# First layer of a two-layer attention and expert kernel: who adds the two parts of the rotation, and who copies the turned sums

## The chip, the cores and the metric

The kernel runs on one core of one Trainium2 chip. The metric is the device time of one execution in microseconds (us). The engines of the core are TensorE (PE in the profile; its weight loads are PEld), VectorE (DVE), ScalarE (ACT), GpSimd (POOL) and SyncE (SP, which here only issues DMAs). Each engine works through its own list of instructions in order; they wait for each other through semaphores.

## The reference: what is computed

The input is 16 sequences ("batches") of 512 tokens with 128 channels, float32. Two layers follow, each of the form `x = x + attention(layernorm(x)) + ffn(layernorm(x))`:

```
layer 1 attention: q, k, v = xn Wq', xn Wk', xn Wv'   (16 heads of 8 channels)
                   q, k = rope(q), rope(k);  q, k = elu(q)+1, elu(k)+1
                   y_t = q_t (sum_{s<=t} k_s v_s') / max(q_t . sum_{s<=t} k_s, 1e-6);   y Wo'
layer 1 ffn:       router softmax over 8 experts, the best two, weights renormalised,
                   squared-ReLU expert MLPs (128-512-128), plus one shared MLP
layer 2 attention: softmax attention over chunks of 64 with a gate from a two-step dynamics
layer 2 ffn:       token-shifted blend, squared ReLU, sigmoid gate
```

The change touches only layer 1's attention. The rotation (rope) of the projected queries and keys is computed as `x * cos + swapped(x) * sin`, where `swapped(x)` comes from a second projection with permuted weights. Its sum goes on to `elu(.)+1`, computed as `max(x, 0) + exp(-relu(-x))`. The attention output carries a ninth column for each head, the denominator; the quotient of the two is what is multiplied by Wo.

## The kernel before, in words

The program has three stages: the first layer over 16 batches (some 16 equal rounds, from about 42 us to 511 us), the expert tiles, and the second layer. Only the first stage is of interest here. In it all engines run a software pipeline: `body(b, first, last)` of each engine is called for b = 0 to 15, and while batch b's attention is computed, the front of batch b+1 (projection, rotation, feature map, router) and the layer norm of batch b+2 are mixed in. The order on each engine is written out by hand; nothing else plans it.

**TensorE, in the order of one round b** (line numbers of the profile): scores of sheet 0 (L1760; a sheet is a group of heads), the wide part of sheets 0 and 1 (`attend_wide`, L1779), the turn of `xn` of b+1 (L1688), half of the output projection of b-1 (L1851, L1852), scores 1, values of sheet 0 (`attend_narrow`, L1788), projections of q for b+1 (L1703, L1704), scores 2, values 1, projections of k for b+1, scores 3, the other half of the projection of b-1, v of b+1 (L1713), wide part of sheets 2 and 3, values 2, turn of k (`turn_k`, L1734), turn of the first attention sums (`turn_oT(b, 0)`, L1820), `sum_states` (L1745), values 3, the shared MLP's first product in four parts (L1837), between which stand `turn_oT(b, 1)` (L1820), `prefix` of the router (L1725) and `turn_y` (L1826).

**VectorE**: `cut` multiplies the scores of four PSUM banks by the causal mask (L1198, four instructions for each sheet); `rotate(b+1, c)` comes after the cuts of sheets 1 (c = 0, queries) and 2 (c = 1, keys): two products out of PSUM (L1071, L1073) and then their sum `t1 + t2` in SBUF (L1076, 128x512 float32). After the cut of sheet 3 comes `feature` (L1095, twice), which needs ScalarE's exponential of the sum; then `residual`, `logits_out`, `router_max`, `ln(b+2)` (L1065), `router`, `y_out(b, 0)` (L1203), `states` (L1084), `router_pick`, `y_out(b, 1)` (L1203), `normalise` (L1209 to L1213) and `slots`. `y_out` copies the turned sums from PSUM bank W7 to `yb` in SBUF, 128x288 float32; `normalise` needs both halves and makes `y`, which TensorE's `turn_y` waits for. The next `prefix` in TensorE's list also waits for both halves (L1721), since it writes to W7.

**ScalarE**: `evac_xnT`, `exps(b+1, 0)` (L809 and L811: the two activations behind the rotation's sum, waiting for semaphore `rot`), `evac_oT(b, 0)`, `exps(b+1, 1)`, `evac_v`, two of `sheets_of_k`, `exp_router`, `evac_ktok` (L860), two more of `sheets_of_k`, `evac_oT(b, 1)` (L840), and four times `square_h` (L850 ReLU, L854 square), with `evac_yT` before the last.

**GpSimd**: eight indirect DMAs a round write the normalised rows of batch b to the experts' places (`scatter`, L687), two after the first scores of the round, two after `pv_done` says that values 0 are done; then `ln_root(b+2)` (L667 to L679, seven small instructions; not issued for the last two batches); then two scatters after values 1, and two at the end of the round's scores. `ln(b+2)` on VectorE overwrites `xn` of batch b, so it waits until all eight scatters of b have landed:

```
if not early(n, 2) and first_layer:
    dve.wait_ge(scattered[n.p], n.own(16 * 2 * J, 0))      # L1063
```

The functions that the diff touches, and what calls them:

Of the kernel before, what the change touches and what calls it, by code (L numbers as in the profile page):

```python
# [9 lines left out]
ALU = mybir.AluOpType  # L10
# [5 lines left out]
H, DH = 16, 8  # L16
E, FF = 8, 512
NB = FF // 128
J = T // 128
CHUNK = 64  # L20
SHEETS, G = 4, 4
PAIRS, TWO = SHEETS // 2, 2
# [84 lines left out]
def build(nc, io, out):  # L107
    ctx = ExitStack()
    with ctx:
# [20 lines left out]
        OT, W5, W6, W7 = bank[4], bank[5], bank[6], bank[7]  # L130
# [186 lines left out]
        def early(b, d):  # L317

            return b.less(d)
# [336 lines left out]
        def _(pool):  # L656
# [24 lines left out]
            def scatter(n, ks):  # L681

                written = value(pool, n.at(1, 1))
                pool.wait_ge(consts_loaded, 16 * CONSTS)
                pool.wait_ge(slots_ready, written)
                for k in ks:
                    nc.gpsimd.indirect_dma_start(  # L687
                        xs_d[:, :], bass.IndirectOffsetOnAxis(ap=idx[n.p][:, k:k + 1], axis=0),
                        xn[n.p][:, k % J, :], None).then_inc(scattered[n.p], 16)

            def body(b, first, last):
                pool.wait_ge(a_ps, b.at(H, G))
                scatter(b, range(0, 2))
                pool.wait_ge(pv_done, b.at(SHEETS, 1))
                scatter(b, range(2, 4))
                if b.known() + 2 < B:
                    ln_root(b + 2)
                pool.wait_ge(pv_done, b.at(SHEETS, 2))
                scatter(b, range(4, 6))
                pool.wait_ge(a_ps, b.at(H, H))  # L700
                scatter(b, range(6, 2 * J))

# [92 lines left out]
        def _(act):  # L795
# [40 lines left out]
            def evac_oT(b, a):  # L836
# [2 lines left out]
                    act.wait_ge(oTT_ps, b.at(PAIRS, a - 1))  # L839
                nc.scalar.copy(oT[a][:, :], OT[:, :]).then_inc(oT_sb, 1)  # L840

            def evac_yT(b, first_layer=True):
                act.wait_ge(yT_ps, b.at(1, 1))
                nc.scalar.copy(yT[:, :], (OT if first_layer else W6)[:, :]).then_inc(yT_sb, 1)  # L844
# [24 lines left out]
            def body(b, first, last):  # L869
                if not last:  # L870
                    evac_xnT(b + 1)
                    exps(b + 1, [0])
                evac_oT(b, 0)
                if not last:
                    exps(b + 1, [1])
                    evac_v(b + 1)
                    sheets_of_k(b + 1, range(2))
                    exp_router(b + 1)
                    evac_ktok(b + 1)
                    sheets_of_k(b + 1, range(2, SHEETS))  # L880
                evac_oT(b, 1)
                for k in range(NB):
                    square_h(b, k)
                    if k == 2 and not last:
                        evac_yT(b)

# [149 lines left out]
        def _(dve):  # L1036
# [31 lines left out]
            def rotate(n, c):  # L1068

                dve.wait_ge(qk_ps, n.at(2, c + 1))  # L1070
                nc.vector.tensor_tensor(t1[c][:, :], W5[:, :], rope[:, 0, :], ALU.mult).then_inc(rot_cos, 1)  # L1071
                dve.wait_ge(qkp_ps, n.at(2, c + 1))
                nc.vector.tensor_tensor(t2[c][:, :], W6[:, :], rope[:, 1, :], ALU.mult).then_inc(rot_sin, 1)  # L1073
                dve.wait_ge(rot_cos, n.at(2, c + 1))
                dve.wait_ge(rot_sin, n.at(2, c + 1))
                nc.vector.tensor_tensor(t1[c][:, :], t1[c][:, :], t2[c][:, :], ALU.add).then_inc(rot, 1)  # L1076

            def states(n):

# [307 lines left out]
            def body(b, first, last):  # L1387
                more = b.known() + 2 < B
                if last:
                    counts()  # L1390
                cut(b, 0)
                if more:
                    dve.wait_ge(x_loaded[b.p], (b + 2).own(16, 16))
                    ln_moments(b + 2)
                slot_weights(b)
                if last:
                    bounds(0)
                    inside(0)
                cut(b, 1)
                if not last:  # L1400
                    rotate(b + 1, 0)
                cut(b, 2)
                if last:
                    row_terms(0)
                    expert_terms()
                if not last:
                    rotate(b + 1, 1)
                cut(b, 3)
                if last:
                    first_tiles()  # L1410
                if not last:
                    feature(b + 1)
                if not first:
                    residual(b + -1)
                if not last:
                    logits_out(b + 1)
                    router_max(b + 1)
                if more:
                    ln(b + 2)
                if not last:  # L1420
                    router(b + 1)
                y_out(b, 0)
                if not last:
                    states(b + 1)
                    router_pick(b + 1)
                y_out(b, 1)
                if not last:
                    normalise(b)
                    slots(b + 1)
# [784 lines left out]
```

## Time and profile before

| | us |
|---|---|
| median of 3 runs (1529.15 to 1532.43) | 1532.0 |
| the profiled execution's own time | 1530.86 |
| its span | 1529.0 |
| TensorE busy in the span | 1415.1 (93%) |
| VectorE busy | 1179.3 (77%) |
| ScalarE busy | 818.9 (54%) |
| GpSimd busy | 524.4 (34%) |

Times in the rows are us from the start of the span, durations are us unless marked ns, and `xN` is a count. A row of a timeline gives start, duration, engine, line, operation, output and input, and in brackets how long the engine was idle before it and what ended that. The ends of matmuls are modelled, so neighbouring PE rows overlap: the distance from start to start tells more than the duration. PEclk is the granted clock of TensorE as a share of 2.4 GHz.

### The profile page before, as it was taken

Reading aid. Unit: us, or ns where it says so; the run is one execution under the profiler, and the core shown is the slowest. Engines: PE = TensorE matmul, PEld = TensorE weight load, DVE = VectorE, ACT = ScalarE, POOL = GpSimd, SP = SyncE. Lnnn points to the kernel's source line nnn. Section 1 sums busy time; section 2 is a strip of 40 time slices with the busy share of each in tenths; the row PEclk is TensorE's granted clock in tenths of the full one; section 3 lists DMA queues with packets and bytes.
Section 4 is the critical chain, followed back from the end, with each engine's and each line's share of the span. In section 5 each row is a group of like instructions: output and inputs, shape, how many; then the busy total and the mean of one; then the engine's idle time right before and its main releaser. Section 6 shows DMA issues by size and latency. Waiting matters only on the chain.

```text
span 1529.0 us, 35462 instructions
## 1 busy us (share of the span) xinstructions
PE 1415.1 (93%) x12938; PEld 914.1 (60%) x12952; DVE 1179.3 (77%) x2690; ACT 818.9 (54%) x1565; POOL 524.4 (34%) x943
## 2 busy tenths in 40 slices
PE   3899999999998799999998999999999999999994
PEld 1667667667677699998885444444444444444432
DVE  3899889889888496456677788888888888888752
ACT  2344434534533333334434677777667777776672
POOL 2343333333233011162412244444444444442121
PEclk8899999999998899999999999999999999999996
DMA  4111111111111566776974343343344443432300
GB/s 121 40 42 56 47 40 58 45 42 56 38 37 36 160 211 209 213 249 209 269 201 78 91 104 99 93 105 93 85 102 105 103 101 94 104 89 71 81 9 14
DMA packets 119084, 152.86 MB, mean 100 GB/s; under 512 B 31348, under 2 KB 83700, under 8 KB 114292
## 3 DMA queue, kind: packets, MB, share of 16 engines
q1 hardware_dynamic: 105992, 120.25, 28.9%
q0 software_dynamic: 12928, 30.43, 6.9%
q8 instruction: 101, 1.65, 0.5%
q14 instruction: 63, 0.52, 0.1%
HBM read 109.01 MB, written 41.09 MB: 98 GB/s over the span
## 4 chain that ended last, share of the span: by engine, by line
PE 49%; DVE 32%; POOL 6%; issue 5%; ACT 5%; SPq 2%; DMA 1%; POOLq 0%; DVEq 0%; ACTq 0%
PE bank L1935 8%; PE bank L1926 8%; DVE P L1198 8%; DVE nmax L1503 8%; PE bank L1803 5%; PE bank L1981 5%; PE bank L2004 4%; ACT P L939 3%; PE bank L1760 2%; PE bank L1837 2%; PE bank L1944 2%; PE bank L1851 2%; DVE t L1073 1%; DVE t L1071 1%; PE bank L2051 1%
## 5 line engine op out<-in xcount | busy, mean ns | idle before, releaser
L1503 DVE TENSOR_REDUCE nmax<-bank 128x1 f32<-128x512 f32 (+3 forms) x704 | 428.6, 633 | 87.7 <-PE bank L1981 86.9
L939 ACT ACTIVATE P<-bank 128x512 f32<-128x512 f32 x640 | 371.3, 599 | 186.0 <-PE bank L2004 179.8
L1981 PE MATMUL bank<-KT,QT 76*128 76x512 bf16 (+3 forms) x1024 | 252.2, 304 | 28.8 <-DVE nmax L1503 20.4
L2004 PE MATMUL bank<-QT,KT 78*128 78x512 bf16 (+3 forms) x1024 | 246.1, 303 | 9.0 <-ACT P L939 5.6
L687 POOL DMA_INDIRECT xs_d<-xn,idx x128 | 124.5, 972 | 308.0 <-PE bank L1760 218.5
L1981 PEld LDWEIGHTS bank<-KT,QT 76*128 76x128 bf16 x1024 | 87.4, 97 | 188.2 <-DVE nmax L1503 129.4
L1803 PE MATMUL bank<-P,V 128*32 128x512 f32 (+3 forms) x2048 | 193.1, 450 | 0.0
L1198 DVE TENSOR_TENSOR P<-bank,early_w 128x512 f32<-128x512 f32 x256 | 158.6, 680 | 37.9 <-PE bank L1760 37.8
L903 ACT ACTIVATE hr<-bank 128x512 f32<-128x512 f32 x144 | 86.0, 597 | 177.9 <-PE bank L1926 174.9
L735 POOL DMA_INDIRECT hT<-ys_d,idx x104 | 103.5, 995 | 162.4 <-PE bank L2004 133.8
L1467 DVE TENSOR_TENSOR hT<-hr 128x512 f32<-128x512 f32 x144 | 98.0, 691 | 68.3 <-ACT hr L903 67.6
L2004 PEld LDWEIGHTS bank<-QT,KT 78*128 78x128 bf16 x1024 | 99.0, 98 | 86.0 <-ACT P L939 30.8
L1935 PEld LDWEIGHTS bank<-P,hT 128*128 128x128 f32 x1152 | 139.0, 192 | 7.4 <-issue 3.0
L1926 PE MATMUL bank<-P 128*128 128x256 f32 x576 | 139.5, 386 | 1.8 <-issue 1.8
L1935 PE MATMUL bank<-P,hT 128*128 128x128 f32 x1152 | 140.5, 275 | 0.7 <-DVE P L1473 0.6
L723 POOL DMA_DIRECT2D ys_d<-P x72 | 52.4, 727 | 225.0 <-DVE P L1473 218.8
L1926 PEld LDWEIGHTS bank<-P 128*128 128x128 f32 x576 | 106.7, 194 | 14.8 <-issue 2.4
L809 ACT ACTIVATE t<-t 128x512 f32<-128x512 f32 x32 | 20.2, 631 | 159.5 <-DVE t L1076 159.5
L1760 PEld LDWEIGHTS bank<-P,QT 32*128 32x128 f32 x2048 | 65.9, 192 | 45.1 <-issue 43.3
L1760 PE MATMUL bank<-P,QT 32*128 32x128 f32 x2048 | 77.8, 290 | 7.6 <-DVE P L1198 7.5
L1803 PEld LDWEIGHTS bank<-P,V 128*32 128x32 f32 x2048 | 40.7, 108 | 64.4 <-issue 49.6
L1851 PE MATMUL bank<-early_w,hT 128*128 128x128 f32 x512 | 70.3, 281 | 1.9 <-ACT yT L844 1.9
(257 smaller groups left out, 2227.2 us busy)
## 6 DMA issues: line engine op xcount, KB each, us to landing
P<-in_fc SPq DMA_DIRECT2D x72, 256.0 KB, 2.9
P<-in_proj SPq DMA_DIRECT2D x72, 256.0 KB, 3.5
QT<-parts_d SPq DMA_DIRECT2D x96, 192.0 KB
parts_d<-parts SPq DMA_DIRECT2D x32, 384.0 KB, 2.7
P<-xs_d SPq DMA_DIRECT2D x72, 128.0 KB, 3.0
ys_d<-P POOLq DMA_DIRECT2D x72, 128.0 KB, 3.6
KT<-parts_d SPq DMA_DIRECT2D x64, 128.0 KB
KT<-parts_d SPq DMA_DIRECT2D x32, 192.0 KB
```

Source lines behind the costliest of these rows:

```text
L687: nc.gpsimd.indirect_dma_start(xs_d[:, :], bass.IndirectOffsetOnAxis(ap=idx[n.p][:, k:k + 1], axis=0), xn[n.p][:, k % J, :], None).then_in ...
L735: nc.gpsimd.indirect_dma_start(gathered_rows(n)[:, k, :], None, rows, bass.IndirectOffsetOnAxis(ap=idx[n.p][:, k:k + 1], axis=0)).then_inc ...
L939: nc.scalar.activation(P[s % 2][:, u, :], bank[k % 2][:, :], ACT.Exp, scale=float(DH) ** -0.5).then_inc(s_sb, 1)
L1198: nc.vector.tensor_tensor(P[s % 2][:, g, :].rearrange("p (j c) -> p j c", c=128), bank[g][:, :].rearrange("p (j c) -> p j c", c=128), tri[ ...
L1503: nc.vector.tensor_reduce(nmax[:, s // TWO, h:h + TWO * nh - 1:TWO, j], max_bank(n, k)[:, 0:nh * w].rearrange("p (h w) -> p h w", h=nh), A ...
L1760: ins = pe.matmul(bank[g][:, tile], kS[b.p][quad, s, tile], qf[b.p][quad, tile], start=True, stop=True)
L1803: ins = pe.matmul(OT[32 * g:32 * g + 32, 128 * kb:T], values(b, kb, s, g), P[s % 2][:, u, c:c + n], start=(s % TWO == 0 and k == 0), stop= ...
L1851: pe.matmul(o, hT[:, j // 2, k, c0:c0 + 128], spj[:, k, :], start=(k == 0), stop=False)
L1926: ins = pe.matmul(w[:, i * GT:(i + 1) * GT], wfc[t.p][:, c * 128:(c + 1) * 128], xgT[t.p % 2], start=True, stop=True)
L1935: ins = pe.matmul(bank[6][:, c * 128:(c + 1) * 128], hT[:, t.p % 2, k, c * 128:(c + 1) * 128], wpj[t.p][:, k, :], start=(k == 0), stop=(k ...
L1981: ins = pe.matmul(max_bank(n, k)[:, i * w:(i + 1) * w], QT[n.p][0:MROWS, h, j * 128:(j + 1) * 128], KT[n.p][0:MROWS, h, 0:w], start=True, ...
L2004: ins = pe.matmul(bank[k % 2][:, c:c + n], KT[b.p][0:SROWS, h, 128 * kb:128 * kb + 128], QT[b.p][0:SROWS, h, 128 * kb:T], start=True, stop ...
```

## The change

`rotate` issues its sum on VectorE for the first batch only. For the others GpSimd does it in `sum_rotation(b+1, c)`: c = 0 behind `ln_root(b+2)`, c = 1 behind the scatters 4 and 5. The copies of the turned sums go to ScalarE: `copy_y(b, 0)` stands behind `evac_ktok(b+1)`, `copy_y(b, 1)` behind the first `square_h` of the round.

```
# GpSimd
+            def sum_rotation(n, c):
+                pool.wait_ge(rot_cos, n.at(2, c + 1))
+                pool.wait_ge(rot_sin, n.at(2, c + 1))
+                nc.gpsimd.tensor_tensor(t1[c][:, :], t1[c][:, :], t2[c][:, :], ALU.add).then_inc(rot, 1)
             def body(b, first, last):
...
                 if b.known() + 2 < B:
                     ln_root(b + 2)
+                if not last:
+                    sum_rotation(b + 1, 0)
                 pool.wait_ge(pv_done, b.at(SHEETS, 2))
                 scatter(b, range(4, 6))
+                if not last:
+                    sum_rotation(b + 1, 1)
                 pool.wait_ge(a_ps, b.at(H, H))
                 scatter(b, range(6, 2 * J))
# ScalarE
+            def copy_y(b, a):
+                act.wait_ge(oTT_ps, b.at(PAIRS, a + 1))
+                nc.scalar.copy(yb[0][...same places...], W7[...]).then_inc(y_sb, 1)
...
                     evac_ktok(b + 1)
+                copy_y(b, 0)
+                if not last:
                     sheets_of_k(b + 1, range(2, SHEETS))
                 evac_oT(b, 1)
                 for k in range(NB):
                     square_h(b, k)
+                    if k == 0:
+                        copy_y(b, 1)
# VectorE
-                dve.wait_ge(rot_cos, n.at(2, c + 1))
-                dve.wait_ge(rot_sin, n.at(2, c + 1))
-                nc.vector.tensor_tensor(t1[c][:, :], t1[c][:, :], t2[c][:, :], ALU.add).then_inc(rot, 1)
+                if early(n, 1):
+                    (the same three lines)
...
-                y_out(b, 0)
                 if not last:
                     states(b + 1)
                     router_pick(b + 1)
-                y_out(b, 1)
```

## Rows read from the trace of the kernel before

**Rows 1.** Busy time by stretch: one round (stretch, length; PE, PEld, DVE, ACT, POOL busy; PEclk, DMA).
```profile
244.32:273.30 28.98, 28.08 (x379) 20.54 (x379) 25.61 (x69) 13.34 (x25) 9.98 (x15) 1.00 0.16 48
```

**Rows 2.** Timeline of TensorE: the end of one round, then the next one.
```profile
241.40 0.49 PE L1725 MATMUL bank<-pickb,before 128*128 128x8 bf16 x14 [0.43 <-DVE yb L1203]
...
242.87 0.66 PE L1826 MATMUL bank<-ident,y 128*128 128x128 f32 x4
...
244.32 1.17 PE L1760 MATMUL bank<-P,QT 32*128 32x128 f32 x32
...
257.26 1.17 PE L1760 MATMUL bank<-P,QT 32*128 32x128 f32 x32 [0.18 <-DVE P L1198]
...
262.39 1.08 PE L1788 MATMUL bank<-P,V 128*32 128x128 f32 x32
263.61 0.52 PE L1734 MATMUL bank<-ident,t 128*128 128x128 f32 x3
...
264.70 1.77 PE L1745 MATMUL bank<-V,P 128*128 128x144 f32 x12
...
268.39 0.63 PE L1820 MATMUL bank<-ident,oT 128*128 128x128 f32 x4
268.86 1.08 PE L1837 MATMUL bank<-xnT,early_w 128*128 128x512 f32 x2
```

**Rows 3.** Timeline of VectorE over the same stretch.
```profile
242.12 0.69 DVE L1213 TENSOR_TENSOR y<-yb,rden 128x512 f32<-128x512 f32 x1
...
245.58 2.48 DVE L1198 TENSOR_TENSOR P<-bank,early_w 128x512 f32<-128x512 f32 x4 [1.88 <-PE bank L1760]
...
258.42 0.69 DVE L1076 TENSOR_TENSOR t<-t 128x512 f32<-128x512 f32 x1
259.03 2.47 DVE L1198 TENSOR_TENSOR P<-bank,early_w 128x512 f32<-128x512 f32 x4
...
262.02 0.68 DVE L1095 SCALAR_TENSOR_TENSOR t<-t,ee 128x512 f32<-128x512 f32 x1
...
263.83 1.11 DVE L1065 TENSOR_SCALAR xn<-xt,mv,rstd 128x128 f32<-128x128 f32 x4
...
268.17 0.60 DVE L1084 TENSOR_TENSOR P<-bank,own 128x432 f32<-128x432 f32 x1
```

**Rows 4.** Timeline of ScalarE over the same stretch.
```profile
259.14 0.63 ACT L809 ACTIVATE t<-t 128x512 f32<-128x512 f32 x1 [2.62 <-DVE t L1076]
...
268.57 0.60 ACT L850 ACTIVATE hr<-bank 128x512 f32<-128x512 f32 x1 [0.44 <-PE bank L1837]
```

**Rows 5.** Timeline of GpSimd over the same stretch.
```profile
256.21 0.20 POOL L679 TENSOR_TENSOR rstd<-rstd,std 128x4 f32<-128x4 f32 x1
256.95 1.03 POOL L687 DMA_INDIRECT xs_d<-xn,idx  x1 [0.54 <-issue]
258.30 0.95 POOL L687 DMA_INDIRECT xs_d<-xn,idx  x1 [0.30 <-issue]
```

**Rows 6.** Groups of GpSimd's instructions by line and shape (busy us, mean ns of one).
```profile
L671 POOL TENSOR_TENSOR std<-std,rstd 128x4 f32<-128x4 f32 x32 | 6.4, 200 | 2.5
...
L428 POOL TENSOR_TENSOR fhn<-fhn 128x64 f32<-128x64 f32 x15 | 4.8, 320 | 1.3
```

**Rows 7.** Timeline near the start: a GpSimd instruction, then the VectorE one beside it.
```profile
20.71 0.54 POOL L679 TENSOR_TENSOR rstd<-rstd,std 128x4 f32<-128x4 f32 x1
...
20.50 0.69 DVE L1076 TENSOR_TENSOR t<-t 128x512 f32<-128x512 f32 x1
```

**Rows 8.** DMA issues by line (count, median us from issue to landing).
```profile
xs_d<-xn,idx POOLq DMA_INDIRECT x128, 2.2
```

**Rows 9.** Timeline of TensorE in round 0.
```profile
59.37 0.52 PE L1734 MATMUL bank<-ident,t 128*128 128x128 f32 x3 [1.71 <-DVE lg L1101]
...
60.96 2.94 PE L1745 MATMUL bank<-V,P 128*128 128x144 f32 x12 [0.63 <-ACT P L860]
```

**Rows 10.** Timeline of TensorE behind the last round.
```profile
506.61 1.16 PE L1851 MATMUL bank<-early_w,hT 128*128 128x128 f32 x8 [1.86 <-ACT yT L844]
```

More of the change, by code:

```diff
@@ L840, in evac_oT @@
                 nc.scalar.copy(oT[a][:, :], OT[:, :]).then_inc(oT_sb, 1)
+            def copy_y(b, a):
+                act.wait_ge(oTT_ps, b.at(PAIRS, a + 1))
+                nc.scalar.copy(yb[0][:, :, TWO * G * a:TWO * G * (a + 1), :].rearrange("p j (g b) c -> p j g (b c)", b=TWO),
+                               W7[:, :].rearrange("p (j g c) -> p j g c", j=J, g=G)[:, :, :, 0:TWO * (DH + 1)]).then_inc(y_sb, 1)
             def evac_yT(b, first_layer=True):
@@ L1073, in rotate @@
                 nc.vector.tensor_tensor(t2[c][:, :], W6[:, :], rope[:, 1, :], ALU.mult).then_inc(rot_sin, 1)
-                dve.wait_ge(rot_cos, n.at(2, c + 1))
-                dve.wait_ge(rot_sin, n.at(2, c + 1))
-                nc.vector.tensor_tensor(t1[c][:, :], t1[c][:, :], t2[c][:, :], ALU.add).then_inc(rot, 1)
+                if early(n, 1):
+                    dve.wait_ge(rot_cos, n.at(2, c + 1))
+                    dve.wait_ge(rot_sin, n.at(2, c + 1))
+                    nc.vector.tensor_tensor(t1[c][:, :], t1[c][:, :], t2[c][:, :], ALU.add).then_inc(rot, 1)
             def states(n):
```

## The prediction

> **What bounds the kernel now.** I first split the span by the busy time of its stretches, then read one round of the first layer in the chain of waits, and last the timeline of each engine over that round. The rounds repeat to a hundredth of a us, so one will do for all: 28.98 us long, at full clock, 2.4 GHz, with TensorE marked busy for 28.08 and VectorE for 25.61 [rows 1]. The reader should see there that both are nearly full: whatever is taken off VectorE can give back only the time in which TensorE waits for it. The chain of waits runs along VectorE from the first cut of a round to the copy of the second half of the turned sums, and along TensorE from there to the next round. TensorE's own waits in a round are few. It waits 0.18 at the fourth scores for a cut, and 0.2 at the turn of k: 262.39 to 263.61 is 1.22, where the same 32 products take 1.01 elsewhere, between neighbours whose starts follow directly. It waits 0.3 at `sum_states`, for ScalarE's copy of the turned k. It waits 0.43 at `prefix`, for the copy in question, and 0.1 at `turn_y` [rows 2]. Together that is some 1.2 to 1.5 us of 28.98. So the largest gain that the change could have, with every wait gone, is 15 rounds by 1.5, 22 us; the question is what new waits it brings.
>
> **What is removed.** VectorE loses two sums of 0.69, with the two waits ahead of each some 0.75 a piece [rows 3], and two copies, which by their effect on the next start are worth 0.38 and 0.47: 2.35 us a round. Its first benefit is at the cuts: the third cut starts at once when its scores are there, so the fourth scores start 0.18 earlier, at 257.08. VectorE's cuts start 1.26 after the scores that they wait for (244.32 to 245.58) and four take 2.4 to the next start, so `feature` for the queries could start at 257.08 + 1.26 + 2.4 = 260.74, where the fourth cut before alone began at 259.03 [rows 2, 3].
>
> **What the GpSimd add costs.** No row shows a 128x512 add there. GpSimd adds 128x4 in 0.20 and multiplies or adds 128x64 in 0.32 [rows 6], which makes 0.12 for 60 elements, 2.0 ns for one, and for 512 elements 0.20 + 508 x 0.0020 = 1.2 us. The bounds are 0.32 (the shorter instruction; below that nothing argues) and 2.2 (twice the slope). I take 1.2 as the line through two rows of the same operation. The Trainium skill, GPSIMD Engine Reference, section 3.1, gives about 2.6 cycles an element at 1.2 GHz for two inputs against VectorE's one; by its figures the add would be an estimated 1.1 us plus the dispatch, close to the value from the rows.
>
> **Where the adds stand.** This is the point of the case. GpSimd's list is in order, and the adds have been put behind work that ends late. `ln_root` ends at 256.41 and the products of the queries' rotation have long been ready, so the first add runs from 256.42 to 257.62. The fourth scatter follows after the same 0.54 as now, at 258.16, the fifth 1.35 later at 259.51, ending at 260.46 [rows 5]. The second add then runs from 260.50 to 261.70. VectorE used to end the same sum at 258.42 + 0.69 = 259.11, and ScalarE took it up at 259.14 [rows 3, 4]. So ScalarE's two activations on the keys, which the list holds ahead of V's copies, start at 261.74 instead of 259.14; their results are there 1.29 later, and VectorE's second `feature` starts at 263.07 instead of 262.02 [rows 3]. That is 1.05 late, although VectorE itself stood ready 1.3 us early. The delay of the queries' sum (by 2.9 us) costs nothing: its exponential is done at some 259.0, before `feature` at 260.74, and `evac_oT(b, 0)` behind it is not needed before TensorE's second wide part, after 261.
>
> **What follows the late feature.** Its chain is residual, logits, the turn of k, ScalarE's sheets and its copy of the turned k, `sum_states`. None of these can start without it, and nothing else in the chain became shorter. TensorE's `turn_k` moves from 263.61 to 264.66 and `sum_states` from 264.70 to 265.75; TensorE, idle before the former for 0.2 now, is idle for about 1.4. `turn_oT(b, 1)` moves from 268.39 to 269.44 and the second shared product could start 0.47 later, at 269.91 [rows 2].
>
> **The scatters' second effect.** GpSimd's scatters 6 and 7 move behind the late add, to 262.24 and 263.50, and scatters land 2.2 after their issue [rows 8]: 265.70. VectorE's `ln(b+2)` waits for them. It would be ready at 263.83 + 1.05 = 264.88 [rows 3], so it waits 0.85 more and is 1.9 late. Here the two removed copies pay: `states` comes at 268.17 + 1.9 - 0.38 = 269.69 and ends at 270.29, which holds the second shared product until 270.35 instead of 269.91; `prefix` is then possible at 271.32.
>
> **The copies on ScalarE.** The first stands in a free stretch and has TensorE's turn long behind it; nothing waits for it but `turn_oT(b, 1)`, 3 us later. The second stands behind the ReLU and the square of the first shared product: the ReLU starts at 268.57 + 1.05 = 269.62 [rows 4], the square ends 1.29 later, the copy takes 0.45 (a 128x288 piece beside the 128x512 ReLU's 0.60; bounds 0.3 and 0.6) and is done at some 271.25. Before, it was done 0.15 ahead of `prefix` (241.40), thus at 270.23 in this round. `prefix` moves from 270.38 to 271.40, and `normalise` behind the copy takes the same 1.56 to the end of `y` (241.25 to 242.81) [rows 2, 3], so `turn_y` and the next round's first scores move by the same 1.05, to within 0.05. The three paths (states, router's pick, copy) arrive nearly together; no second delay adds up.
>
> **The sum.** A round is 1.05 longer. This holds for rounds 0 to 13: 14.7 us. Round 14 has no `ln_root`, and the adds are early: there TensorE loses 0.45 of its waits and still waits for the late copy; I count 0.5 gained. In the last round no rotation is left, and TensorE waits for ScalarE at the end (1.86 before 506.61) [rows 10], whose list is longer by one copy that matters: 0.4 lost. That is 14.6. One more term: in round 0, TensorE stood 1.71 and 0.63 us idle at just these two places, and then its clock fell to 1.2 GHz: `sum_states` took 2.94 instead of 1.77, and the values behind it were longer too, 1.6 together [rows 2, 9]. The changed kernel stands idle for about 1.4 and 0.3 there in each round. That is less, so I expect the fall in few rounds, and count one beyond round 0: 1.6. In all 16.2. The profiled execution took 1530.9 by its own clock (its span is 1529.0), which makes 1547.1; the median of the runs shown is 1.1 above it, 1532.0, which makes 1548.2. Forecast: 1548. Its own range, with the add at 1.0 to 1.4 and none to four falls of the clock, is 1541 to 1556.
>
> **Rivals.**
> 1. VectorE gets in first. An instruction of GpSimd that began 0.21 after VectorE's sum of two SBUF tiles took 0.54 instead of 0.20, ending just behind it [rows 7]: the two exclude each other. Here the second add would begin at 260.50 and `feature` of the queries, with two inputs in SBUF, at 260.74. If the add comes first, `feature` waits, which is harmless. If GpSimd is a quarter us slower, it waits for `feature` until 261.41, and each round is 0.9 longer again: 14 x 1.95 - 0.1 + two falls of the clock 3.2 = 30.4, 1562. For it: the margin is 0.24 with an add that no row shows. Against it: 0.24 is over the scatter of the rows. (The Trainium skill, SBUF — State Buffer, section "Who interferes with whom", says that a VectorE instruction with two SBUF inputs and a GpSimd one that reads SBUF exclude each other and the first holds the port; the trace agrees, by the same 0.54. With the rule as with the row the sum is the same.)
> 2. The clock falls in each round: 14 x (1.05 + 1.6) - 0.1 = 37, 1569. For it round 0 [rows 9], against it that its idle time was 0.6 us longer, and the 1.86 idle before 506.61, behind which eight products took 1.16, no longer than at full clock [rows 10].
> 3. The other side, faster: GpSimd's add is short enough. `feature` of the keys starts at 260.67 plus twice the add; that equals today's 262.02 with an add of 0.67, and from there down the round gets shorter, until at 0.33 TensorE and ScalarE's late copy bind, and a round is 0.5 shorter: 15 x 0.5 = 7.5, 1524. For it: 0.67 is VectorE's own time for the sum. Against it: the two rows' slope makes 1.2, and 0.67 would need less than half of that slope.
> 4. The delays find slack that I missed (the keys' path loses 1.05 but the waits of 0.18, 0.2, 0.43 go), and the time is the same: 1530 to 1534.
>
> **How the numbers follow.** Forecast 0.60; rival 1, 0.12; rival 2, 0.09; rival 3, 0.11; rival 4, 0.08. A measurement of this kernel tells 0.2%, 3 us, from no change. Slower holds the forecast and rivals 1 and 2, 0.81; faster 0.11; same 0.08. The range must leave out no more than 0.2: I let go of rivals 3 and 4, and it reaches up into rival 2: 1538 to 1567.
>
> **What would show it.** In the profile after: GpSimd's add near 1.2 us (step 1); ScalarE's L809 for the keys waiting for POOL, not DVE, and starting some 17.4 us after the round's first scores instead of 14.8 (step 2); VectorE idle before its second `feature`, and idle before `xn` for a DMA; TensorE idle over 1 us before the turn of k; rounds of 30.0 us, and 28.5 for round 14. I am wrong if the add is under 0.7, if the second add begins before the scatters 4 and 5 are through, or if rounds are 31 and more with the clock at 0.5 behind the turn of k.

## The result, and the profile after

The changed kernel took 1548.74 us (median of 4 runs, 1544.8 to 1549.73) against 1532.22 for the kernel before on the same chip (4 runs, 1529.15 to 1533.01): a ratio of 1.011, 95% interval 1.0089 to 1.013. It is slower, by 16.5 us where 16.2 were forecast. The profiled execution has a span of 1548.0 us against 1529.0, 19.0 more. Its busy times are TensorE 1414.6 us, VectorE 1159.5 (19.8 less), ScalarE 826.8 (7.9 more), GpSimd 572.1 (47.7 more).

One round of the changed kernel, as its stretch (the columns are those of [rows 1]; scores to scores):

```profile
252.62:282.75 30.13, 28.00 (x378) 20.64 (x378) 24.38 (x65) 13.78 (x27) 13.02 (x17) 1.00 0.15 45
```

30.13 us instead of 28.98, at the same full clock. VectorE is marked busy for 1.23 us less in it (although one of its products, held by GpSimd's add, counts 0.64 more), TensorE for 0.08 less, and yet the round is 1.15 longer. Now the timeline of TensorE in the same round. To compare with [rows 2], take 8.30 off the starts: that round began at 244.32, this one at 252.62.

```profile
252.62 1.17 PE L1778 MATMUL bank<-P,QT 32*128 32x128 f32 x32
...
265.31 1.17 PE L1778 MATMUL bank<-P,QT 32*128 32x128 f32 x32
...
272.69 0.52 PE L1752 MATMUL bank<-ident,t 128*128 128x128 f32 x3 [1.17 <-DVE lg L1121]
...
273.78 1.77 PE L1763 MATMUL bank<-V,P 128*128 128x144 f32 x12
...
278.77 1.12 PE L1855 MATMUL bank<-xnT,early_w 128*128 128x512 f32 x2 [0.72 <-DVE P L1104]
279.74 0.49 PE L1743 MATMUL bank<-pickb,before 128*128 128x8 bf16 x14
...
281.31 0.65 PE L1844 MATMUL bank<-ident,y 128*128 128x128 f32 x4
...
282.75 1.17 PE L1778 MATMUL bank<-P,QT 32*128 32x128 f32 x32
```

The 0.18 ahead of the fourth scores is gone (265.31), and so is the 0.43 ahead of `prefix` (L1743). Two longer waits stand in their place: 1.17 at the turn of k, and 0.72 at the second shared product, for VectorE's `states` (L1104). VectorE in that stretch:

```profile
268.98 1.32 DVE L1115 SCALAR_TENSOR_TENSOR P<-t,ee 128x512 f32<-128x512 f32 x1
271.09 0.69 DVE L1115 SCALAR_TENSOR_TENSOR t<-t,ee 128x512 f32<-128x512 f32 x1 [0.80 <-ACT ee L821]
...
274.13 1.12 DVE L1084 TENSOR_SCALAR xn<-xt,mv,rstd 128x128 f32<-128x128 f32 x4 [1.14 <-DMA xs_d<-xn,idx]
...
278.11 0.61 DVE L1104 TENSOR_TENSOR P<-bank,own 128x432 f32<-128x432 f32 x1
```

VectorE stands idle twice, for 0.80 and 1.14 us: time that it used to spend on the sums and copies. The GpSimd list that makes it wait, and ScalarE between the two:

```profile
264.68 1.28 POOL L695 TENSOR_TENSOR t<-t 128x512 f32<-128x512 f32 x1
266.12 1.04 POOL L687 DMA_INDIRECT xs_d<-xn,idx  x1 [0.16 <-issue]
267.46 0.96 POOL L687 DMA_INDIRECT xs_d<-xn,idx  x1 [0.31 <-issue]
268.45 1.28 POOL L695 TENSOR_TENSOR t<-t 128x512 f32<-128x512 f32 x1
269.90 1.25 POOL L687 DMA_INDIRECT xs_d<-xn,idx  x1 [0.17 <-issue]
271.46 1.16 POOL L687 DMA_INDIRECT xs_d<-xn,idx  x1 [0.30 <-issue]
```

```profile
269.77 0.63 ACT L819 ACTIVATE t<-t 128x512 f32<-128x512 f32 x1 [2.01 <-POOL t L695]
...
278.82 0.38 ACT L854 COPY yb<-bank 128x288 f32<-128x288 f32 x1
```

The waits of the whole trace, by engine and line (us in total, times, longest), show that this is every round and not this one:

```profile
DVE xn L1084 <- DMA xs_d<-xn,idx: 16.3, 14, 1.6
```

### The profile page after: what moved, and what is told of

Read it like the earlier page. It is cut to its first block, busy times and chain, and to the rows that moved or that the text cites. A ratio compares the mean times of both kernels' runs of the same rounds, so it can differ in the third digit from the quotient of the medians.

```text
span 1548.0 us, 35462 instructions
## 1 busy us (share of the span) xinstructions
PE 1414.6 (91%) x12952; PEld 914.2 (59%) x12952; DVE 1159.5 (75%) x2628; ACT 826.8 (53%) x1597; POOL 572.1 (37%) x973
## 4 chain that ended last, share of the span: by engine, by line
PE 52%; DVE 23%; POOL 10%; issue 5%; ACT 4%; DMA 3%; SPq 2%; POOLq 0%; DVEq 0%; ACTq 0%
DVE nmax L1521 9%; PE bank L1953 8%; PE bank L1944 8%; PE bank L1821 7%; PE bank L1999 6%; PE bank L2022 5%; POOL xs_d L687 4%; PE bank L1778 3%; POOL t L695 2%; ACT P L958 2%; DMA xs_d<-xn,idx 2%; PE bank L1962 2%; PE bank L1869 2%; PE bank L1806 1%; PE bank L2069 1%
## 5 line engine op out<-in xcount | busy, mean ns | idle before, releaser
L687 POOL DMA_INDIRECT xs_d<-xn,idx x128 | 131.9, 1030 | 278.1 <-PE bank L1778 196.8
L1218 DVE TENSOR_TENSOR P<-bank,early_w 128x512 f32<-128x512 f32 x256 | 159.0, 684 | 47.9 <-PE bank L1778 47.7
L1855 PE MATMUL bank<-xnT,early_w 128*128 128x512 f32 x128 | 70.6, 636 | 9.3 <-DVE P L1104 9.3
```

Of the source, the lines that this page charges most:

```text
L687: nc.gpsimd.indirect_dma_start(xs_d[:, :], bass.IndirectOffsetOnAxis(ap=idx[n.p][:, k:k + 1], axis=0), xn[n.p][:, k % J, :], None).then_in ...
L1218: nc.vector.tensor_tensor(P[s % 2][:, g, :].rearrange("p (j c) -> p j c", c=128), bank[g][:, :].rearrange("p (j c) -> p j c", c=128), tri[ ...
```

## Experiments

All ratios are to the kernel before, run in between on the same chip. The kernels ran on three chips, and these differ: before took 1530.79 us on chip 1, 1539.15 on chip 2 and 1541.99 on chip 3. The pair of the result (1532.22) is like chip 1, so the runs there bear on it most directly; what the other chips add of their own is taken up with their runs. The runs on chip 2 came first, and the expectations for chip 1 refer to them.

### On chip 1: before, after, and both late paths taken away

**The kernel before, traced once more.**

> The kernel before itself, for its trace on the chip of these runs. The kernel with the copies alone showed rounds of 29.76 us against 28.98 in the trace of before, and yet took 1.0007 of the time of before on its chip. Theory A (the copies cost 0.78 us a round, and something of like size is saved or spent outside the rounds): here again rounds of 28.98 to 29.0 us, the fourth group of cuts 0.0 us idle. Theory B (a wait of about 0.7 us before the fourth group of cuts, TensorE's scores named, belongs to the execution or the chip and not to the copies): rounds of 29.6 to 29.8 here as well, with that wait in them.

Measured: rounds of 28.96 to 28.99 us, one execution of 1531.5 us, and no wait ahead of the fourth cuts. So the wait seen with the copies alone (below) is not in the kernel before on this chip; for the others the question stays.

**The changed kernel, once more.**

> The changed kernel itself, beside its parts on one chip. Both theories: rounds of 30.13 us in the trace and 1.010 to 1.013 of the time of before. If the adds alone (31.0 us rounds, 1.0098) and the whole change come out the same here, the copies bring nothing.

Measured: 1546.56 us, ratio 1.0107 (1.0086 to 1.0129), rounds of 30.1 us. The result repeats.

**A third buffer of rows, and the second add ahead of scatters 4 and 5.** The buffer lies in a part of `P[1]` that the first layer doesn't use; `ln(b+2)` then waits for the scatters of b-1, long landed.

```
-        xn = [sb(...) for p in range(2)]
+        xn = [sb(...) for p in range(2)] + [P[1][:, UNITS - 1, :].rearrange(...)]
+        rows_of(n): xn[n.known() % 3] in the first layer, xn[n.p] as before behind it
+                                                     # used by scatter, ln and the turn of xn
-                if not early(n, 2) and first_layer:
-                    dve.wait_ge(scattered[n.p], n.own(16 * 2 * J, 0))
+                if not early(n, 3) and first_layer:
+                    old = n + -3
+                    dve.wait_ge(scattered[old.p], old.own(16 * 2 * J, 16 * 2 * J))
...
-                pool.wait_ge(pv_done, b.at(SHEETS, 2))
-                scatter(b, range(4, 6))
                 if not last:
                     sum_rotation(b + 1, 1)
+                pool.wait_ge(pv_done, b.at(SHEETS, 2))
+                scatter(b, range(4, 6))
```

> The whole change, with both late paths taken away: a third buffer of normalised rows, so that the fourth next message's rows wait for no scatter, and the second add ahead of scatters 4 and 5, so that it starts when its products are there. Theory of two late paths (landing of the scatters, and the keys' activation behind the second add): with both gone the round is 28.5 us, as round 14 was, and the time 0.993 to 0.997 of before. Rival (moving the second add forward is itself what cost in the kernel with that edit alone, through ScalarE's wait of 2.2 us ahead of the copy of the key tokens, 1.0178): that wait shows here too and rounds are 30 to 31 us, 1.010 to 1.018.

Measured: 1523.22 us (7 runs), ratio 0.9957 (0.9941 to 0.9973), rounds of 28.50 to 28.52. As the theory of the two late paths said, to 0.02 us a round. One round, then GpSimd and TensorE in it:

```profile
267.75:296.26 28.51, 27.85 (x378) 20.56 (x377) 23.56 (x65) 13.86 (x27) 12.93 (x17) 1.00 0.17 49
```

```profile
281.51 1.28 POOL L699 TENSOR_TENSOR t<-t 128x512 f32<-128x512 f32 x1 [0.43 <-DVE t L1097]
282.95 1.03 POOL L691 DMA_INDIRECT xs_d<-P,idx  x1 [0.16 <-issue]
```

```profile
293.27 0.49 PE L1748 MATMUL bank<-pickb,before 128*128 128x8 bf16 x14 [0.43 <-ACT yb L858]
```

The add now waits for VectorE's products and not for scatters, and what TensorE waits for is the copy of the turned sums on ScalarE, the one that the change put there. The same list of instructions on every engine but for one swap on GpSimd, and one more buffer, is the difference between 1.1% slower and 0.4% faster.

**The same, with the second copy between the first ReLU and its square.**

```
# square_h(b, k) on ScalarE
                 nc.scalar.activation(hr[k % 2][:, :], ..., ACT.Relu).then_inc(h_relu, 1)
+                if k == 0:
+                    copy_y(b, 1)
                 act.wait_ge(h_relu, b.at(NB, k + 1))
# body
-                    if k == 0:
-                        copy_y(b, 1)
```

> The kernel with both late paths taken away, and ScalarE's second copy of the turned sums between the first ReLU and its square instead of behind the square, 0.63 us earlier. If what then sets the round is the copy, the denominators, y and its turning, the round is 27.9 to 28.0 us and the time 0.988 to 0.992 of before. If the round is then set by something else (the scores and cuts of the next sheet), it is as the kernel with both edits, 28.5 us. If the rival on the moved add holds, 30 to 31 us as there.

Measured: 1513.87 us (4 runs), ratio 0.9896 (0.9874 to 0.9918), rounds of 27.84 to 27.85: the best kernel of the study, 17 us faster than before. A round, and VectorE's wait for the copy in it, which was 1.16 in the kernel above:

```profile
262.28:290.13 27.85, 27.70 (x378) 20.62 (x378) 23.55 (x65) 13.73 (x27) 12.93 (x17) 1.00 0.17 50
```

```profile
278.64 0.68 DVE L1120 SCALAR_TENSOR_TENSOR P<-t,ee 128x512 f32<-128x512 f32 x1
...
287.10 0.22 DVE L1234 TENSOR_SCALAR den<-yb 128x64 f32<-128x64 f32 x1 [0.51 <-ACT yb L858]
```

The place of one copy of 0.39 us in ScalarE's list is worth 0.66 a round (28.51 to 27.85): the 0.63 of the square ahead of it. TensorE is now marked busy for 27.70 of 27.85.

### On chip 2: one part at a time

**The copies alone, the adds back on VectorE.**

```
-                if early(n, 1):
+                if early(n, 1) or c in (0, 1):      # rotate: the sum on VectorE
...
-                if not last:
-                    sum_rotation(b + 1, 0)          # GpSimd; likewise (b + 1, 1)
```

> Half of the change: the turned sums are copied by ScalarE as in the changed kernel, both rotation sums stay on VectorE. Theory (the GpSimd adds cost the time, the copies nothing): the second copy ends at about the time at which VectorE used to end it (0.1 us earlier by the rows of before), so a round stays 28.9 us against 28.97, and the time is 1530 to 1532. Rival (ScalarE's late copy holds prefix and turn_y): rounds of 29.5 or more, 1540 and up.

Measured: 1540.49 us (12 runs), ratio 1.0007 (0.9992 to 1.0023), rounds of 29.76. The ratio says "no difference", as the theory had it; the rounds are 0.86 longer than its 28.9 and, like the bare time, those of the rival. VectorE in this trace, and the GpSimd scatter that waits for the same scores:

```profile
264.27 0.69 DVE L1092 TENSOR_TENSOR t<-t 128x512 f32<-128x512 f32 x1
265.69 2.48 DVE L1214 TENSOR_TENSOR P<-bank,early_w 128x512 f32<-128x512 f32 x4 [0.73 <-PE bank L1774]
265.99 0.96 POOL L687 DMA_INDIRECT xs_d<-xn,idx  x1 [0.89 <-PE bank L1774]
...
276.89 0.22 DVE L1225 TENSOR_SCALAR den<-yb 128x64 f32<-128x64 f32 x1 [0.85 <-ACT yb L850]
```

The fourth cuts wait 0.73 for scores that began at 263.11. In the changed kernel such a cut begins 1.26 after its scores, here 2.58, in every round. GpSimd's scatter 6 waits for these scores too, and it stood idle for 0.89, where in the kernel before it followed its neighbour after 0.30. So by the trace two engines got TensorE's signal late, and the delay is not VectorE's own. The rival, that ScalarE's late copy holds `prefix`, doesn't explain it: TensorE waits 0.43 there, as before.

**The adds alone, the copies back on VectorE.**

```
-                copy_y(b, 0)                        # ScalarE; likewise copy_y(b, 1)
...
+                y_out(b, 0)                         # VectorE, behind router(b + 1)
...
+                y_out(b, 1)                         # VectorE, behind router_pick(b + 1)
```

> The other half: GpSimd adds the rotation's two parts as in the changed kernel, the copies of the turned sums stay on VectorE. Theory: VectorE's chain behind the layer norm binds (it waits for the scatters to land), and it has the two copies back in it, 0.38 and 0.47 us, so a round is 0.85 to 0.9 us longer than in the changed kernel, 31.0 us instead of 30.13: 14 times that is 12 us, 1560 to 1562, unless TensorE's clock falls more often. Rival (the late feature alone binds, through turn_k, sum_states and the copy): VectorE has slack there and the time stays at that of the changed kernel, 1549. Rival (the copies are what costs): 1532 to 1536.

Measured: 1555.31 us (6 runs), ratio 1.0098 (1.0077 to 1.0119), rounds of 30.9 to 31.0. The round is as expected: the adds do the harm, and without the copies' removal from VectorE's list it is 0.83 more than the changed kernel's. The time is 5 us below the 1560 to 1562 expected, and 16 us above before, where 14 rounds by 2.0 would be 28.

**The third buffer alone** (`xn`, `rows_of` and the wait as shown on chip 1; the order of GpSimd's list as in the changed kernel).

> The changed kernel with a third buffer for the normalised rows in the first layer, so that the layer norm of b+2 waits for the scatters of b-1 and not of b. The wait of 1.14 us before xn goes. Theory: two paths are late, the scatters' landing by 0.5 us more than the keys' feature. With the first gone the second binds, with ScalarE's second copy behind it: prefix starts 26.7 us after the round's first scores instead of 27.1, a round is 29.65 us instead of 30.13, and the time 6 to 7 us less than the changed kernel's, 1542. Rival (only the landing costs): rounds of 28.5 us, 1526. Rival (only the late feature costs): no change, 1549.

Measured: 1541.66 us (12 runs), ratio 1.0012 (0.9997 to 1.0027), rounds of 29.70, both as the theory of two late paths had them (29.65, 1542). With the landing of the scatters out of the way, TensorE waits at the turn of k and at `prefix`:

```profile
239.12 0.52 PE L1757 MATMUL bank<-ident,t 128*128 128x128 f32 x3 [1.15 <-DVE t L1120]
...
245.77 0.49 PE L1748 MATMUL bank<-pickb,before 128*128 128x8 bf16 x14 [0.43 <-ACT yb L858]
```

So in the changed kernel the landing is the later path by 0.43 us a round (30.13 less 29.70), and behind it, almost as late, comes the keys' path through the second add. The two traces are from different chips, but `sum_states` begins 21.15 us after a round's first scores here and 21.16 there, so they can be compared.

**The second add moved ahead alone.**

> The changed kernel with GpSimd's second add moved ahead of scatters 4 and 5. It then starts when the keys' products are ready, 13.6 us after the round's first scores, and ScalarE has the exponential done before the fourth cut ends, so feature waits for nothing and turn_k comes at its natural 18.85 us. GpSimd's work stays the same, so the last scatter is issued at 18.85 and lands at 21.1 to 21.5. Theory: the layer norm still starts at 21.2 to 21.5 and the round stays within 0.4 us of 30.13 although the late feature is gone: 1543 to 1549. Rival (the late feature is the cause): rounds of 28.5 us and 1526.

Measured: 1568.07 us (5 runs), ratio 1.0178 (1.0153 to 1.0202), rounds of 30.9 to 31.1 and five behind the first of 32.0 to 34.3. Worse than the changed kernel, where the theory had 1543 to 1549 and the rival 1526: both missed. That the turn of k comes in time and the rows still wait for the landing was foreseen. This was not:

```profile
247.57 0.95 POOL L687 DMA_INDIRECT xs_d<-xn,idx  x1 [0.30 <-issue]
249.50 0.48 ACT L875 COPY P<-bank 128x384 f32<-128x384 f32 x1 [2.24 <-remote]
250.03 1.77 PE L1763 MATMUL bank<-V,P 128*128 128x144 f32 x12 [1.93 <-ACT P L875]
250.42 1.12 DVE L1084 TENSOR_SCALAR xn<-xt,mv,rstd 128x128 f32<-128x128 f32 x4 [3.43 <-DMA xs_d<-xn,idx]
...
255.06 1.12 PE L1855 MATMUL bank<-xnT,early_w 128*128 128x512 f32 x2 [0.75 <-DVE P L1104]
```

ScalarE's copy of the key tokens starts 2.24 us late, though the turn of k that it needs began at 246.97 and took 0.55. The trace names no engine of this core as the releaser ("remote"). But this wait is not what makes a round 30.9. The last scatter is issued 19.44 us after the round's first scores instead of 18.84, since the second add, now ahead of four scatters, has to wait 0.53 for VectorE's products; the rows are written at 22.29 instead of 21.51, and the next round begins at 30.91 instead of 30.13, late by the same 0.78, with TensorE waiting for `states` once more (255.06). The landing path alone accounts for these rounds. The wait on ScalarE costs something in others: in four of the five long ones the granted clock is 0.66 between 21.8 and 26.8 us after the first scores, so a part of that ran at 1.2 GHz, behind some 2 us in which TensorE stood idle for that copy. In the longest, and in part in the one behind it, the rows waited longer for the landing (5.51 and 4.65).

### On chip 3

**The copies alone, again.**

> The kernel with the copies alone, once more. Its first trace had rounds of 29.76 us, 0.78 longer than before, through a wait of 0.7 us ahead of the fourth group of cuts that names the scores, and yet its time was 1.0007 of before. Theory A (the wait belongs to this kernel): rounds of 29.76 us again, and a time of 1.000 only if the chip of the first run had a slower before, so that here the ratio is 1.007. Theory B (the wait came with that chip or execution, and what the copies do by themselves is move the denominators by nothing: VectorE is freed 0.9 us early and waits for ScalarE): rounds of 28.9 to 29.0 us and 0.998 to 1.001 of before.

Measured: 1540.54 us (12 runs), ratio 0.9992 (0.9981 to 1.0002), rounds of 29.7, the wait ahead of the fourth cuts 0.66. Neither theory has this pair: the rounds are those of theory A, the ratio is that of theory B.

**Both copies on ScalarE, the second between ReLU and square, the adds on VectorE.**

> The adds on VectorE as before, both copies of the turned sums on ScalarE, the second one between the first ReLU and its square. By the trace of before, the output's first copy starts 21.97 us into the round; the second copy of the turned sums would start 1.5 later and the denominators at 24.0 instead of 24.69, so that the round is 28.3 us and the time 0.993 to 0.995 of before. If the wait of 0.7 us ahead of the fourth cuts belongs to kernels with these copies, the round is 29.0 to 29.1 us and the time 1.000 to 1.002.

Measured: 1529.92 us (6 runs), ratio 0.992 (0.9901 to 0.994), rounds of 29.04. Again the ratio that belongs to no wait, with the rounds that belong to a wait (0.68 ahead of the fourth cuts):

```profile
285.84 1.17 PE L1774 MATMUL bank<-P,QT 32*128 32x128 f32 x32 [0.18 <-DVE P L1214]
...
288.36 2.48 DVE L1214 TENSOR_TENSOR P<-bank,early_w 128x512 f32<-128x512 f32 x4 [0.68 <-PE bank L1774]
```

What follows: against the copies alone on the same chip, the new place is worth 0.65 us a round and 10.6 us, as on chip 1 (0.66 and 9.4). The copies pay by themselves once the second stands there, by 0.8%. And the reading that fits all runs on chips 2 and 3 is that the wait of 0.7 us also sits in the kernel before there, with rounds of some 29.7: that makes before 14 x 0.7 = 10 us slower than on chip 1 (measured 8.4 and 11.2). Measured against rounds of 29.7 instead of 28.98, the copies alone should cost 0 (measured +1.3 and -1.5), this kernel -9 (-12.1), the adds alone +18 (+16.2), the third buffer 0 (+2.5). For the three kernels with uneven rounds, rounds 0 to 14 together give +29 for the second add ahead (+28.9), +31 for it again (+25.8; its traced run was 7.7 us above its median), and +15 for the clearing below (+12.0). A second sign points the same way. What lies outside rounds 0 to 14 takes 1093.9 and 1094.5 us in the two traces of before, and 1089.2 to 1097.9 in the eight traces from chips 2 and 3. That part is not longer on those chips, so what before takes more there has to be looked for in the rounds. This is inferred, not shown: neither chip has a trace of before.

**The second add ahead, again.**

> The changed kernel with the second add ahead of scatters 4 and 5, once more. The first time it was 1.0178 of before, with a wait of 2.2 us ahead of ScalarE's copy of the key tokens in every round, which the kernel with a third buffer of rows besides didn't show (28.5 us a round). Theory A (the wait belongs to this order with two buffers): 30.9 to 31.1 us a round and 1.015 to 1.020 again, with the 2.2 us in every round. Theory B (it came with the chip or the execution): the copy of the key tokens is on time, the rows wait 3.4 us for the scatters' landing, and rounds are 30.5 to 31.1 us by the landing path alone, the copy's idle time 0 to 0.3 us.

Measured: 1567.81 us (5 runs), ratio 1.016 (1.0135 to 1.0185), rounds of 30.9 to 32.2 behind a first one of 36.4. The wait is there again, here between 100 and 420 us, ten rounds:

```profile
ACT P L875 <- remote: 20.4, 10, 2.1
```

2.0 us a round on a second chip, in 14 of 15 rounds: it comes with this kernel on chips 2 and 3, not with one execution. The rows wait for the landing by 3.4 us in most rounds, so both of what theory A and theory B named is there. The rounds of 30.9 are again those of the landing path, and in five of the longer ones the granted clock is 0.66 at the same place. The kernel with the third buffer besides has 0.29 at that copy, but ran on chip 1. Which of the two took the wait away, the buffer or the chip, is open.

**GpSimd busy for a moment ahead of the second add**, so that VectorE's product should reach the port first.

```
                 if not last:
+                    nc.gpsimd.memset(P[1][:, UNITS - 2:UNITS, :].rearrange(...)[:, 0:704], 0.0)
                     sum_rotation(b + 1, 1)
```

> The changed kernel, and GpSimd clears 704 elements of each row of a buffer that isn't in use, ahead of the second add, so that VectorE's product for the queries has the port before the add asks for it. The clearing is work that the kernel doesn't need. In the changed kernel the add had the port first: 1.28 us for the add and 1.32 instead of 0.68 for the product. Theory (the two exclude each other, and who comes first has it for its whole instruction): the product takes 0.68 us, the add is recorded 0.5 to 0.6 us longer or later, the keys' activation starts 1 to 1.2 us later than in the changed kernel, the round is 31.2 us and the time 1.020 to 1.024 of before. Rival (GpSimd always comes first, or the two share it evenly): the product takes 1.0 to 1.3 us again, the add 1.28, and the time is under 1.020.

Measured: 1553.98 us (6 runs), ratio 1.0081 (1.0061 to 1.01), rounds of 30.74. The order was not turned round:

```profile
272.44 0.70 POOL L709 MEMSET P<- 128x704 f32 x1
...
273.10 1.28 POOL L695 TENSOR_TENSOR t<-t 128x512 f32<-128x512 f32 x1
273.27 1.67 DVE L1116 SCALAR_TENSOR_TENSOR P<-t,ee 128x512 f32<-128x512 f32 x1
```

The clearing took 0.70, and VectorE's product came 0.17 after the add instead of before it. So the case in which VectorE is first was not reached, and the kernel shows another thing: the add began 0.66 later, and the round is 0.61 longer than the changed kernel's 30.13 (in its two traces, from chips where before takes 1531 to 1532 us; it was not run on chip 3). As far as these can be compared, the second add's start carries through to the round almost one to one, by the scatters behind it: the last is issued 19.47 us after the round's first scores instead of 18.84, and the rows are written at 22.12 instead of 21.51.

## Why the prediction was right, and where only by luck

With the 8.30 us taken off, the steps against the trace after:

| step | forecast | measured |
|---|---|---|
| GpSimd add | 1.2 | 1.28 |
| second add | 260.50 to 261.70 | 260.15 to 261.43 |
| `feature` of the keys | 263.07 | 262.79 |
| turn of k; TensorE idle | 264.66; 1.4 | 264.39; 1.17 |
| `sum_states` | 265.75 | 265.48 |
| scatters 6 and 7 | 262.24, 263.50 | 261.60, 263.16 |
| `ln(b+2)`; wait | 265.73; 0.85 | 265.83; 1.14 |
| `states` | 269.69 | 269.81 |
| second shared product | 270.35 | 270.47 |
| second copy done | 271.25 | 270.90 |
| `prefix` | 271.40 | 271.44 |
| next round's first scores | 274.35 | 274.45 |

**The removed work** (2.35 us a round) gave little, as said: the fourth scores came 0.25 earlier (265.31 less 8.30, against 257.26) where 0.18 was forecast, and the waits behind them took it back.

**The add** was 1.28 (thirty of them, 1.267 to 1.297) for 1.2 by the line through 128x4 and 128x64 [rows 6]. Rival 3 needed 0.67 or less and is out. So is rival 4, which let the waits of 0.18 and 0.43 pay for the delay: they went, and 1.17 and 0.72 came.

**Where the add stands** was the cause, as said. The gap between an add and the scatter behind it is 0.17 and not the 0.54 carried over from behind `ln_root` [rows 5]; that made the keys' path 0.3 less late than forecast. One number beside it was wrong without harm: the prediction has VectorE ready 1.3 us early, but that is the first `feature` held against the second. First against first, 260.74 and 261.42, it is 0.68.

**The landing** was under-priced on the other side. Two scatters behind the second add took 1.25 and 1.16 instead of the 0.96 that the step allowed, and the rows could be written 2.67 after the last issue, not 2.2 [rows 8]. The last issue was itself 0.34 earlier than forecast, so `ln` began only 0.10 later; that it waited 1.14 instead of 0.85 is for the rest because it was ready 0.19 sooner.

**What is last.** The prediction let three paths arrive nearly together and named ScalarE's copy as last, `states` 0.08 ahead of it. The trace has it the other way: the copy (0.38, forecast 0.45) is done at 270.90, and TensorE waits at the second shared product for `states`. (The prediction's own terms for the copy, 269.62 + 1.29 + 0.45, make 271.36 and not the 271.25 that it went on with; by them the round would have been 0.1 longer, for a path that wasn't the last.) The kernel with the third buffer measures both: without the landing the round is 29.70, so the keys' path and the copy are worth 0.72 above before, and the landing another 0.43. Forecast 1.05 for the former alone, and nothing more from the latter. The mechanism was right, two terms were off by 0.33 and 0.43 with opposite signs, and the round is 1.15 instead of 1.05 longer.

**The sum.** First cuts to first cuts, round 0 is 1.37 longer (30.53 against 29.16) and rounds 1 to 13 together 15.05, 16.4 for which 14.7 were counted. What round 0 adds differs from one execution to the next, since the clock fell in it in the kernel before and in the changed kernel of the result, but not in the changed kernel's second trace, from chip 1, with the same waits ahead. First the result's, then the other's:

```profile
61.71 2.62 PE L1763 MATMUL bank<-V,P 128*128 128x144 f32 x12 [0.64 <-ACT P L875]
```

```profile
61.71 1.77 PE L1763 MATMUL bank<-V,P 128*128 128x144 f32 x12 [0.64 <-ACT P L875]
```

On chip 1 round 0 is 0.46 longer than before and not 1.37. Round 14 is 28.50 us long, to the hundredth what was forecast, but that is no gain of 0.5: the kernel before has no `ln` in it either and takes 28.32 there, from 447.15 to 475.47, a row that the prediction didn't look at. The change costs 0.18 in it, 0.7 worse than counted. The last round, from its first scores to the last projection behind it, takes 32.61 instead of 31.14. On chip 1, where the clock fell at the same place in both kernels, it is 0.41 longer, the size forecast for ScalarE's list. The other 1.06 here is the clock: it came back sooner from the fall early in the round (the scores at 506.62 took 1.17, in before 2.09), and it fell a second time in a place where before had none, the one fall that was counted at 1.6. First the changed kernel, then before:

```profile
514.97 0.63 PE L1838 MATMUL bank<-ident,oT 128*128 128x128 f32 x4 [3.07 <-DVE xr L1239]
...
516.62 2.07 PE L1855 MATMUL bank<-xnT,early_w 128*128 128x512 f32 x2
...
524.72 1.16 PE L1869 MATMUL bank<-early_w,hT 128*128 128x128 f32 x8 [1.87 <-ACT yT L859]
```

```profile
498.51 0.63 PE L1820 MATMUL bank<-ident,oT 128*128 128x128 f32 x4 [0.92 <-DVE xr L1219]
500.08 1.12 PE L1837 MATMUL bank<-xnT,early_w 128*128 128x512 f32 x2
```

Two shared products took 2.07 instead of the 1.12 at full clock, so 1.2 GHz, behind 3.07 us in which TensorE stood idle; before, it stood 0.92 at this place, and its clock was already back from a fall earlier in the round. In the steady rounds, idle for 1.17 and 0.72, the clock stayed at 1.00, which disposes of rival 2 for this kernel. (With some 2 us idle at that place, in the kernel with the second add ahead, it fell in some rounds.) What lies behind 524.72 is 0.9 longer than what lay behind [rows 10]; no step accounts for it, and on chip 1 the same stretch is 3.7 shorter in the changed kernel (1019.7 against 1023.3), so a single trace doesn't settle a difference of that size. The steps came out 1.7 low for rounds 0 to 13 and 0.7 low for round 14, and 0.5 high for the clock. With the 0.9 that makes 19.0 in the profiled pair, and 16.5 between the medians. That the forecast of 16.2 meets the latter to 0.3 us is better than the steps deserve.

**Rival 1** was near, and on the harmless side. The product of the queries started 0.53 behind the add and took 1.32 instead of 0.68, ending 0.57 after the add's end. (The Trainium skill, SBUF — State Buffer, section "Who interferes with whom", has a VectorE instruction with two SBUF inputs and a GpSimd one that reads SBUF exclude each other, the first holding the port; the trace agrees, by these 1.32 us.) Its price, with VectorE first, was not measured.

## What to carry to other kernels

Offloading work to an idle engine is priced by its place in that engine's list, not by its duration: here the same add cost 1.1% behind two scatters, and beside a third buffer and one place earlier it paid 0.4%, with the copy moved by one instruction 1.0%. A transfer issued later for it, and the buffer that it frees, is the second path to follow; take both away together, since undoing one shows only the other. And when chips differ by half a per cent, trace the kernel before on the chip of each comparison, or the rounds in the traces and the ratios of the times will contradict each other.

## What the runs showed of the hardware

- VectorE's product with two SBUF inputs, caught by a GpSimd add, ends 0.55 to 0.57 us after the add does, wherever in the add it began. In the changed kernel it started 0.53 after the add and took 1.32; with the clearing ahead 0.17 and 1.67; in the kernels with the adds alone and with the third buffer alone 0.82 and 1.02. This holds in all 68 cases of five traces. The record begins early, and the product stands still until the add is done. In the best kernel the add is over in time, and it takes 0.68.
- For an indirect scatter the order decides as well. The 191 scatters between 72 and 480 us of the fourteen traces that began while VectorE ran a 128x512 instruction with two SBUF inputs took 1.14 to 1.41. The 130 inside which such an instruction began later took 0.95 or 0.96, as in [rows 5], where the one at 258.30 has VectorE's sum of 258.42 in it [rows 3]. The others took 0.95 to 1.04, but for two (1.15 and 1.54). So an offload that shifts GpSimd's list against VectorE's also changes what the scatters in it cost.
- Before takes 8 to 11 us more on two of the three chips, and one wait may be the reason: in the kernels with the sums on VectorE the fourth cuts began 2.5 to 2.6 us after their scores on chips 2 and 3, where the changed kernel of the result has 1.26 and the kernel before 1.8. With the sums on GpSimd they began 1.23 to 1.48 after on those chips. Why is open.
- ScalarE's wait of 2.0 to 2.3 us ahead of the copy of the key tokens, in 29 of 30 rounds of one kernel on two chips, with no releaser of this core named, is open as well.
